# Attention and a gated MLP on one core: transposing the probabilities by VectorE and memory in place of TensorE

## The chip, the cores and the metric

One core of one Trainium2 chip runs the whole program. The metric is the device time of one execution in microseconds (us). The engines named below are TensorE (PE; its weight loads are PEld), VectorE (DVE), ScalarE (ACT), GpSimd (POOL) and SyncE (SP), which here only issues transfers.

## What is computed

Input x has 16 sequences of 256 tokens with 256 features. A layer norm, causal attention with 16 heads of 128 features, a layer norm of its result and a residual add give x1; a layer norm, a gated MLP with dequantised 4-bit weights, a layer norm and a residual add give the output. All of it is fp32.

```
q = einsum(norm(x), W_Q) + b_Q      # k and v likewise
scores = where(causal, q @ k.T / sqrt(128), -100000)
attn = softmax(scores)
z = attn @ v
x1 = x + norm(einsum(z, W_O) + b_O)
gate, up = norm(x1) @ Wg.T, norm(x1) @ Wu.T     # Wg, Wu, Wd = nibble table x scale
out = x1 + norm((gelu(gate) * up) @ Wd.T)
```

## The kernel before

The 4096 tokens are worked in 8 chunks of 512 tokens, two sequences (b = 0, 1) each. Attention is a loop over 8 chunks and 16 heads, 128 steps; then the MLP is a loop over 8 chunks and 16 tiles of its hidden width. Products are made from two fp32r parts of each operand, a high one (rounded) and a low one (the rest): `three` (L487) issues high x high, high x low, low x high. So every operand is split after it is made: ScalarE writes the high part from PSUM, VectorE the low part (the `full` helpers: high at L370 and L372, low at L667 and L669).

The order of the attention loop is the table that `step_plan` (L63) writes; every engine walks through the same table and does its share of each entry. Step j of a chunk holds: q and k of head j + 1; pT, the transposition of head j's probabilities by TensorE, three 128x128 blocks for each b, (L581) into PSUM, split by ScalarE (L445) and VectorE (L831); in steps 0, 4, 8 and 12 the v projections of four heads (four token tiles of 24 products in all); out, the product of head j - 1 with W_O, summed in two PSUM banks over all heads; the scores of head j + 1 (L510, L513 and `three`); and z of head j. Causality leaves three of four 128x128 blocks of scores for each b: queries 0 to 127 with keys 0 to 127, queries 128 to 255 with all keys. In z the early keys meet all 256 queries, the late keys the late 128 queries.

After the scores VectorE adds the mask, scales and takes the row maximum (`mask_scores`, L675 and L679), ScalarE takes the exponentials with their sums (`exps`, L378 and L380), VectorE inverts the sums (L686) and GpSimd multiplies (`normalise`, L953). Both b have one tile of probabilities each, `probs[b]`.

Beside this VectorE has other work at fixed places (`extra`): in steps 1, 3, 5, 7, 9 and 11 it turns nibbles into MLP weights (L736 to L753; the scaling L753 stands behind z's low part), in others it takes the statistics of the next chunk, standardises the last chunk's attention output and adds its residual. ScalarE and GpSimd split these weights too (L392, L947), and ScalarE's queue stores them. The transposes of the next chunk's x (xT, L504) come in step 14. At a chunk's end VectorE takes the summed output from PSUM (L848).

In the first chunk GpSimd splits the attention weights as they come, in 32 pairs of 256 KB (`PAIRS`, both parts on GpSimd, L973 and L975) through two buffers; SP loads a pair when the one before the last is split. SP's queue also loads and stores x, and in the last chunk it loads the dequantised weights.

PSUM: three banks in rotation for q, k, z, v and xT (`fbank`), three for scores and transposed probabilities (`ubank`), two for out (`obank`).

## Time and profile before

| | us |
|---|---|
| median of 3 runs (1725.49 to 1727.16) | 1726.49 |
| the profiled execution | 1724.96 |
| its span | 1723.1 |
| PE busy | 1690.0 (98%) |
| DVE busy | 1210.9 (70%) |
| ACT busy | 928.3 (54%) |
| POOL busy | 518.3 (30%) |
| granted TensorE clock, share of full speed | 0.998 |

The profile is of one execution on the chip. Times in it are us from the start of the span unless marked ns. A matmul's busy time reaches into the next one's, since they are pipelined; the distance of two starts is what an instruction costs. "idle before" is the engine's own idle time just ahead of an instruction, with the engine and line that ended it.

### The profile page before, as it was taken

How to read it: one execution, taken by the hardware profiler on the slowest of the kernel's cores; microseconds unless marked ns; L12 is line 12 of the kernel's file. 1: busy time of each engine (PE TensorE's matmuls, PEld its weight loads, DVE VectorE, ACT ScalarE, POOL GpSimd, SP SyncE). 2: the span in 40 equal slices, each digit the busy share in tenths (PEclk: the TensorE clock that was granted, in tenths of full speed). 3: DMA queues.
4: the chain of work that ended last, by engine and by line, in shares of the span. 5: the costliest groups of instructions: out<-in, count | busy, mean ns of one | idle time of the engine just before them, and what ended most of it. 6: DMA issues, size and time to landing. Idle time of an engine off the chain costs nothing.

```text
span 1723.1 us, 29141 instructions
## 1 busy us (share of the span) xinstructions
PE 1690.0 (98%) x10624; PEld 1506.7 (87%) x10624; DVE 1210.9 (70%) x3488; ACT 928.3 (54%) x2273; POOL 518.3 (30%) x825
## 2 busy tenths in 40 slices
PE   6999999999999999999999999999999999999997
PEld 5998899889899889988989988998888888888886
DVE  5777777777777677777778767876565565566564
ACT  3665566565566556656656656664444444444443
POOL 6662222222122222212212212223333333333332
PEclk9999999999999999999999999999999999999999
DMA  3220011010001001101100102242000000100000
GB/s 118 84 85 22 14 50 32 10 47 20 19 22 50 22 13 50 32 10 47 32 7 22 50 22 86 88 162 73 13 25 22 29 25 13 37 25 13 25 25 13
DMA packets 60239, 67.05 MB, mean 39 GB/s; under 512 B 4672, under 2 KB 53952, under 8 KB 60096
## 3 DMA queue, kind: packets, MB, share of 16 engines
q1 hardware_dynamic: 32832, 46.30, 8.5%
q10 hardware_dynamic: 27264, 18.89, 3.4%
q8 instruction: 85, 1.39, 0.3%
q14 instruction: 58, 0.48, 0.1%
HBM read 44.20 MB, written 20.97 MB: 38 GB/s over the span
## 4 chain that ended last, share of the span: by engine, by line
PE 97%; DVE 1%; ACT 1%; issue 0%; POOL 0%; DMA 0%; POOLq 0%; DVEq 0%; ACTq 0%
PE fbank L488 17%; PE fbank L490 17%; PE fbank L489 17%; PE obank L488 7%; PE obank L489 7%; PE obank L490 7%; PE ubank L488 6%; PE ubank L489 5%; PE ubank L490 5%; PE ubank L581 5%; PE ubank L510 2%; PE ubank L513 1%; PE fbank L504 1%; DVE v_lo L667 0%; DVE zT_lo L669 0%; DVE stream L700 0%
## 5 line engine op out<-in xcount | busy, mean ns | idle before, releaser
L953 POOL TENSOR_SCALAR probs<-probs,rsum 128x128 f32<-128x128 f32 (+1 forms) x512 | 216.7, 437 | 727.0 <-DVE rsum L686 722.0
L488 PE MATMUL fbank<-xnT_hi,weights 128*128 128x512 f32 x768 | 310.5, 404 | 1.4 <-DVE xnT_lo L667 1.4
L490 PE MATMUL fbank<-xnT_hi,weights 128*128 128x512 f32 x768 | 304.4, 396 | 0.0
L489 PE MATMUL fbank<-xnT_lo,weights 128*128 128x512 f32 x768 | 303.9, 396 | 0.0
L378 ACT ACTIVATE probs<-probs,nmax 128x128 f32<-128x128 f32 x256 | 101.0, 394 | 252.1 <-DVE nmax L679 252.1
L404 ACT ACTIVATE w_raw<-fbank 128x512 f32<-128x512 f32 x128 | 76.5, 597 | 265.2 <-PE fbank L490 265.2
L490 PEld LDWEIGHTS fbank<-xnT_hi,weights 128*128 128x128 f32 x768 | 144.5, 188 | 34.6
L488 PEld LDWEIGHTS fbank<-xnT_hi,weights 128*128 128x128 f32 x768 | 145.1, 189 | 25.4 <-DVE xnT_lo L667 1.8
L777 DVE SCALAR_TENSOR_TENSOR w_raw<-w_raw,fbank 128x512 f32<-128x512 f32 x128 | 87.9, 687 | 111.7 <-ACT w_raw L404 111.6
L489 PEld LDWEIGHTS fbank<-xnT_lo,weights 128*128 128x128 f32 x768 | 145.2, 189 | 23.8
L783 DVE SCALAR_TENSOR_TENSOR probs<-w_raw,fbank 128x512 f32<-128x512 f32 x128 | 87.9, 687 | 97.6 <-ACT w_raw L408 97.6
L488 PE MATMUL obank<-wo_hi,zT_hi 128*128 128x256 f32 x512 | 151.7, 296 | 2.4 <-DVE zT_lo L669 2.4
L489 PE MATMUL obank<-wo_lo,zT_hi 128*128 128x256 f32 x512 | 143.3, 280 | 0.0
L490 PE MATMUL obank<-wo_hi,zT_lo 128*128 128x256 f32 x512 | 143.0, 279 | 0.0
L489 PE MATMUL fbank<-pT_lo,v_hi 128*128 128x256 f32 (+1 forms) x512 | 142.5, 278 | 0.0
L490 PE MATMUL fbank<-pT_hi,v_lo 128*128 128x256 f32 (+1 forms) x512 | 142.1, 278 | 0.0
L667 DVE TENSOR_TENSOR v_lo<-fbank,v_hi 128x512 fp32r<-128x512 f32 x128 | 88.5, 691 | 73.8 <-ACT v_hi L370 73.6
L488 PE MATMUL fbank<-pT_hi,v_hi 128*128 128x256 f32 (+1 forms) x512 | 137.4, 268 | 2.7 <-DVE v_lo L667 2.3
L990 POOL TENSOR_TENSOR qT<-probs,qT 128x512 fp32r<-128x512 f32 x64 | 82.9, 1295 | 176.5 <-ACT qT L413 176.5
L372 ACT ACTIVATE kT<-fbank,bias_k 128x512 fp32r<-128x512 f32 x128 | 88.0, 688 | 87.3 <-PE fbank L490 87.3
L669 DVE SCALAR_TENSOR_TENSOR kT<-fbank,bias_k,kT 128x512 fp32r<-128x512 f32 x128 | 96.1, 750 | 53.2 <-ACT kT L372 51.7
L669 DVE SCALAR_TENSOR_TENSOR zT_lo<-fbank,bias_v,zT_hi 128x512 fp32r<-128x512 f32 x128 | 96.1, 750 | 50.5 <-ACT zT_hi L372 50.4
(109 smaller groups left out, 4946.1 us busy)
## 6 DMA issues: line engine op xcount, KB each, us to landing
w_raw<-in_w_pairs SPq DMA_DIRECT2D x32, 256.0 KB, 2.7
weights<-w_hi_scratch SPq DMA_DIRECT2D x8, 768.0 KB, 4.8
weights<-w_lo_scratch SPq DMA_DIRECT2D x8, 768.0 KB, 6.6
x_in<-in_x SPq DMA_DIRECT2D x8, 512.0 KB, 3.8
x_res<-in_x SPq DMA_DIRECT2D x8, 512.0 KB, 5.6
x_scratch<-stream SPq DMA_DIRECT2D x8, 512.0 KB, 3.2
x_in<-x_scratch SPq DMA_DIRECT2D x8, 512.0 KB, 3.8
x_res<-x_scratch SPq DMA_DIRECT2D x8, 512.0 KB, 4.6
```

Of the source, the lines that this page charges most:

```text
L372: ins = act.activation(dst, bank, ACT.Identity, bias=bias)
L378: act.activation(pr[:, 0:P], pr[:, 0:P], ACT.Exp, bias=nmax[:, 0:1], scale=-1.0, accum_out=sums[:, 0:1])
L488: nc.tensor.matmul(out, a[0], b[0], start=start, stop=False, skip_group_check=skip)
L489: nc.tensor.matmul(out, a[0], b[1], start=False, stop=False, skip_group_check=skip)
L490: return nc.tensor.matmul(out, a[1], b[0], start=False, stop=stop, skip_group_check=skip)
L581: last = nc.tensor.transpose(bank[:, t * P:(t + 1) * P], pr[:, t * P:(t + 1) * P], mem.ident[:])
L667: ins = dve.tensor_tensor(dst, bank, hi.bitcast(F32), ALU.subtract)
L669: ins = dve.scalar_tensor_tensor(dst, bank, bias, hi.bitcast(F32), ALU.add, ALU.subtract)
L777: dve.scalar_tensor_tensor(mem.th[j % 2], mem.th[j % 2], 1.0 / GELU_A, mem.gbank[slot(j)][:], ALU.add, ALU.mult).then_inc(s.arg, 1)
L783: after(dve.scalar_tensor_tensor(act_v, mem.th[j % 2], 1.0, mem.gbank[slot(j)][:], ALU.add, ALU.mult))
L953: last = pool.tensor_scalar(pr[:, lo:hi], pr[:, lo:hi], mem.rsum[i][b][:, part:part + 1], 1.0, ALU.mult, ALU.mult)
L990: pool.tensor_tensor(lo, mem.act_v[j % 2], hi.bitcast(F32), ALU.subtract).then_inc(s.iT_lo, 1)
```

## The change

`step_plan` is now numbered over all 128 steps (n = 16 x chunk + head), and one part step is added at the end. Step n holds: q of head n + 1; **T** of head n; k of head n + 1; pT of head n - 1; out of head n - 2; the scores of head n + 1; z of head n - 1; then the v projections. So z and the sum into out come one step later than before, and the scores stand ahead of z and v.

T: VectorE turns each 32x32 block of `probs[b]` (128x384, twelve blocks) into the tile `turned[b]`. SP stores it to memory and, when the store has landed, loads it back in four transfers for each b, one for each group of 32 partitions, in runs of 96 numbers, so that the blocks also change places (`send_around`). `back` has two buffers for each b. pT: ScalarE copies the early keys (256 columns) to the high part, GpSimd writes the low part, both from SBUF. The late keys (128 columns) are used from `back` as they are, in fp32, with `v_late`, an fp32 copy of v's late token tiles; one fp32 product takes the place of three fp32r products. VectorE no longer writes a low part for these tiles or for pT.

Also: the high parts of the attention weights are made by ScalarE and only the low ones by GpSimd; the pairs are in another order and are spread over the steps 0 to 13, two a step, behind four at the start; `x1_norm`'s roots and two residual parts are moved; a nibble tile has one buffer where it had two; the residual, x and weight transfers of SP stand between the round trips; the MLP's first tiles are rearranged.

```diff
-def step_plan(c, j):
+def step_plan(n):
...
-    plan = [("gu", 0)] if last else [("q", j + 1), ("k", j + 1)]
-    plan += [("pT", j)]
-    if j == HEADS - 2:
+    plan = [("q", n + 1), ("T", n), ("k", n + 1)]
+    if n > 0:
+        plan += [("pT", n - 1)]
+    if n % HEADS == HEADS - 2:
         plan += [("xT", 0)]
-    if j % HG == 0:
+    if n > 1:
+        plan += [("out", n - 2)]
+    if n % HEADS == HEADS - 2:
+        plan += [("xT", 1)]
+    plan += [("scores", n + 1)]
+    if n > 0:
+        plan += [("z", n - 1)]
+    if n % HG == 0:
         plan += [("v", t) for t in range(TT)]
...
+    def send_around(n):
+
+        i = n % 2
+        for b in range(2):
+            if n >= 2:
+                sp.wait_ge(s.back[b], 64 * (n - 1))
+            sp.wait_ge(s.turned[b], n + 1)
+            sp.dma_start(turned_v[i][b].rearrange("a i k c -> (a i) k c"),
+                         mem.turned[b][:].rearrange("p k u j -> p k (u j)")).then_inc(s.sent[b], 16)
+        if n >= 2:
+            sp.wait_ge(s.full, nth(("z", n - 2)))
+        for b in range(2):
+            sp.wait_ge(s.sent[b], 16 * (n + 1))
+            for k in range(4):
+                sp.dma_start(mem.back[i][b][32 * k:32 * k + 32].rearrange("p a u j -> p a (u j)"),
+                             turned_v[i][b][:, :, k].rearrange("a i c -> i a c")
+                             ).then_inc(s.back[b], 16)
...
+    for n in range(STEPS_ALL):
+        c, j = n // HEADS, n % HEADS
+        send_around(n)
+        for pair in pairs_of_step(n + 1):
+            load_pair(pair)
+        if c and j == 8:
+            finish(c)
...
         elif kind == "pT":
             for b in range(2):
-                u = 2 * (c * HEADS + m) + b
-                act.wait_ge(s.pT, u + 1)
-                act.activation(mem.pT[b][0][:], mem.ubank[u % UB][:, 0:384],
+                act.wait_ge(s.back[b], 64 * (m + 1))
+                act.activation(mem.pT[b][0][:].rearrange("p (u a j) -> p u a j", a=4, j=32),
+                               mem.back[m % 2][b][:, :, 0:2, :].rearrange("p a u j -> p u a j"),
                                ACT.Copy).then_inc(s.pT_hi, 1)
+            for pair in pairs_of_step(n):
+                weights_hi(pair)
...
                 if u >= UB:
-                    pe.wait_ge(s.pT_lo, u - UB + 1)
+                    pe.wait_ge(s.masked, u - UB + 1)
                 scores(u, h % 2, b)
-        elif kind == "pT":
-            for b in range(2):
-                u = 2 * (c * HEADS + m) + b
-                bank, pr = mem.ubank[u % UB], mem.probs[b]
-                pe.wait_ge(s.probs, u + 1)
-                for t in range(3):
-                    last = nc.tensor.transpose(bank[:, t * P:(t + 1) * P], pr[:, t * P:(t + 1) * P],
-                                               mem.ident[:])
-                last.then_inc(s.pT, 1)
...
-                three(bank[:, o:o + SEQ], [p[:, 2 * b, e0:e0 + E] for p in mem.v],
-                      [p[:, 0:SEQ] for p in mem.pT[b]], True, False)
-                last = three(bank[:, o + P:o + SEQ], [p[:, 2 * b + 1, e0:e0 + E] for p in mem.v],
-                             [p[:, SEQ:384] for p in mem.pT[b]], False, True)
+                three(bank[:, o:o + SEQ], [p[:, b, e0:e0 + E] for p in mem.v],
+                      [p[:] for p in mem.pT[b]], True, False)
+                last = nc.tensor.matmul(bank[:, o + P:o + SEQ].rearrange("p (a j) -> p a j", j=32),
+                                        mem.v_late[:, b, e0:e0 + E], mem.back[m % 2][b][:, :, 2, :],
+                                        start=False, stop=True)
...
-        elif kind == "pT":
+        elif kind == "T":
             for b in range(2):
-                u = 2 * (c * HEADS + m) + b
-                dve.wait_ge(s.pT_hi, u + 1)
-                dve.tensor_tensor(mem.pT[b][1][:], mem.ubank[u % UB][:, 0:384],
-                                  mem.pT[b][0][:].bitcast(F32), ALU.subtract).then_inc(s.pT_lo, 1)
-            if last_head:
-                gated(0, 0)
+                dve.wait_ge(s.probs, 2 * m + b + 1)
+                if m:
+                    dve.wait_ge(s.sent[b], 16 * m)
+                dve.transpose(mem.turned[b][:].rearrange("p k u j -> p u k j"),
+                              mem.probs[b].rearrange("p (u k j) -> p u k j", u=3, k=4)
+                              ).then_inc(s.turned[b], 1)
```

How the rows move. VectorE, a step with nibble work (head 1), from the second inverted sum on, before:

```order
L686 RECIPROCAL rsum<-sums 128x2
L669 SCALAR_TENSOR_TENSOR zT_lo<-fbank,bias_v,zT_hi 128x512
L753 SCALAR_TENSOR_TENSOR w<-spread,scale 128x128 x2
L669 SCALAR_TENSOR_TENSOR qT<-fbank,bias_q,qT 128x512
L669 SCALAR_TENSOR_TENSOR kT<-fbank,bias_k,kT 128x512
L831 TENSOR_TENSOR pT_lo<-ubank,pT_hi 128x384 x2
```

and with the change:

```order
L788 RECIPROCAL rsum<-sums 128x2
L771 SCALAR_TENSOR_TENSOR zT_lo<-fbank,bias_v,zT_hi 128x512
L855 SCALAR_TENSOR_TENSOR w<-spread,scale 128x128 x2
L771 SCALAR_TENSOR_TENSOR qT<-fbank,bias_q,qT 128x512
L935 STREAM_TRANSPOSE turned<-probs 128x3x4x32 x2
L771 SCALAR_TENSOR_TENSOR kT<-fbank,bias_k,kT 128x512
```

The two operations on the probabilities stand between q's and k's low parts, where they stood behind k's. TensorE, one batch half of z and the first product of the next q, before:

```order
L488 MATMUL fbank<-pT_hi,v_hi 128x256
L489 MATMUL fbank<-pT_lo,v_hi 128x256
L490 MATMUL fbank<-pT_hi,v_lo 128x256
L488 MATMUL fbank<-pT_hi,v_hi 128x128
L489 MATMUL fbank<-pT_lo,v_hi 128x128
L490 MATMUL fbank<-pT_hi,v_lo 128x128
L488 MATMUL fbank<-xnT_hi,weights 128x512
```

and with the change:

```order
L595 MATMUL fbank<-pT_hi,v_hi 128x256
L596 MATMUL fbank<-pT_lo,v_hi 128x256
L597 MATMUL fbank<-pT_hi,v_lo 128x256
L695 MATMUL fbank<-back,v_late 128x128
L595 MATMUL fbank<-xnT_hi,weights 128x512
```

Three products of 128 columns have become one. SP's queue in a step of the first chunk, with the change (before, such a step held the w_raw transfers alone):

```order
L398 DMA turned_scratch<-turned 128x384 [waits probs0_turned,turned0_back]
L398 DMA turned_scratch<-turned 128x384 [waits probs1_turned,turned1_back]
L405 DMA back<-turned_scratch 32x4x96 [waits turned0_stored,full_ready]
L405 DMA back<-turned_scratch 32x4x96 x3
L405 DMA back<-turned_scratch 32x4x96 [waits turned1_stored]
L405 DMA back<-turned_scratch 32x4x96 x3
L380 DMA w_raw<-in_w_pairs 128x512 [waits w_split] x2
```

Ten transfers of a round trip stand ahead of the pair loads.

## Rows read from the trace of the kernel before

**Rows 1.** Page, part 1 (busy us, share, instructions) and part 4 (chain by engine)
```profile
PE 1690.0 (98%) x10624; PEld 1506.7 (87%) x10624; DVE 1210.9 (70%) x3488; ACT 928.3 (54%) x2273; POOL 518.3 (30%) x825
...
PE 97%; DVE 1%; ACT 1%; issue 0%; POOL 0%; DMA 0%; POOLq 0%; DVEq 0%; ACTq 0%
```

**Rows 2.** Timeline of one step; start us, us, engine, line, operation, names, shape, [idle <-releaser]
```profile
826.70 0.28 PE L510 MATMUL ubank<-kT,qT 128*128 128x256 f32 x1
...
827.87 0.29 PE L488 MATMUL fbank<-pT_hi,v_hi 128*128 128x256 f32 x1
...
828.22 0.22 PE L488 MATMUL fbank<-pT_hi,v_hi 128*128 128x128 f32 x1
...
828.51 0.33 PE L488 MATMUL fbank<-pT_hi,v_hi 128*128 128x256 f32 x1
...
829.20 0.45 PE L488 MATMUL fbank<-xnT_hi,weights 128*128 128x512 f32 x1
...
830.83 0.75 DVE L669 SCALAR_TENSOR_TENSOR zT_lo<-fbank,bias_v,zT_hi 128x512 fp32r<-128x512 f32 x1 [0.25 <-ACT zT_hi L372]
...
831.50 0.48 DVE L753 SCALAR_TENSOR_TENSOR w<-spread,scale 128x128 f32<-128x128 f16 x2
...
831.90 0.74 DVE L669 SCALAR_TENSOR_TENSOR qT<-fbank,bias_q,qT 128x512 fp32r<-128x512 f32 x1
832.04 0.82 PE L581 MATMUL ubank<-ident,probs 128*128 128x128 f32 x6
832.25 0.69 ACT L372 ACTIVATE kT<-fbank,bias_k 128x512 fp32r<-128x512 f32 x1 [0.71 <-PE fbank L490]
...
832.62 0.36 PE L488 MATMUL obank<-wo_hi,zT_hi 128*128 128x256 f32 x1
...
832.97 0.75 DVE L669 SCALAR_TENSOR_TENSOR kT<-fbank,bias_k,kT 128x512 fp32r<-128x512 f32 x1 [0.32 <-ACT kT L372]
...
834.12 0.28 PE L510 MATMUL ubank<-kT,qT 128*128 128x256 f32 x1
```

**Rows 3.** Two windows, 16 steps and one v step; columns: stretch, us, busy (count), clock, DMA
```profile
683.48:826.70 143.22, 142.53 (x939) 128.59 (x938) 109.41 (x362) 85.67 (x232) 34.09 (x74) 1.00 0.10 29
841.53:854.46 12.93, 12.93 (x78) 11.35 (x77) 9.65 (x30) 7.28 (x18) 3.67 (x7) 1.00 0.07 21
```

**Rows 4.** Timeline, a step without nibble work
```profile
819.27 0.28 PE L510 MATMUL ubank<-kT,qT 128*128 128x256 f32 x1
...
824.15 0.75 DVE L669 SCALAR_TENSOR_TENSOR qT<-fbank,bias_q,qT 128x512 fp32r<-128x512 f32 x1
```

**Rows 5.** Groups of instructions by form; busy us, mean ns of one, idle before
```profile
L831 DVE TENSOR_TENSOR pT_lo<-ubank,pT_hi 128x384 fp32r<-128x384 f32 x256 | 129.5, 547 | 0.3 <-ACT pT_hi L445 0.3
...
L975 POOL TENSOR_TENSOR weights<-w_raw,weights 128x512 fp32r<-128x512 f32 x24 | 31.2, 1302 | 2.0
```

**Rows 6.** Timeline of the start
```profile
20.89 0.75 DVE L669 SCALAR_TENSOR_TENSOR kT<-fbank,bias_k,kT 128x512 fp32r<-128x512 f32 x1 [0.62 <-ACT kT L372]
...
21.70 0.39 PE L510 MATMUL ubank<-kT,qT 128*128 128x256 f32 x1 [1.56 <-DVE kT L669]
...
40.41 0.28 PE L510 MATMUL ubank<-kT,qT 128*128 128x256 f32 x1
```

**Rows 7.** Timeline where one chunk ends and the next begins
```profile
727.03 0.37 PE L510 MATMUL ubank<-kT,qT 128*128 128x256 f32 x1
...
727.95 0.69 DVE L667 TENSOR_TENSOR xnT_lo<-fbank,xnT_hi 128x512 fp32r<-128x512 f32 x1 [0.67 <-ACT xnT_hi L370]
...
740.59 1.27 DVE L848 TENSOR_TENSOR stream<-obank,bias_o 128x512 f32<-128x512 f32 x2
```

**Rows 8.** DMA issues: what, queue, count, KB each, median us from issue to landing
```profile
w_raw<-in_w_pairs SPq DMA_DIRECT2D x32, 256.0 KB, 2.7
...
w_lo_scratch<-w_0lo ACTq DMA_DIRECT2D x24, 128.0 KB, 2.3
```

**Rows 9.** Timeline of SP's queue at the start
```profile
1.22 0.96 SPq L319 DMA_DIRECT2D w_raw<-in_w_pairs  x2
```

More of the change, by code:

```diff
@@ new lines, with whole, full_key @@
+STEPS = [(n, kind, m) for n in range(STEPS_ALL + 1) for kind, m in step_plan(n)]
+FULLS = ("q", "k", "v", "z", "xT")
+LAST_Z = ("z", STEPS_ALL - 1)
+def whole(kind, m):
+    return kind == "v" and m % 2 == 1
+def full_key(n, kind, m):
+    if kind == "xT":
+        return (kind, n // HEADS + 1, m)
+    if kind == "v":
+        return (kind, n // HG, m)
+    return (kind, m)
+def full_places():
+    place = {("xT", 0, 0): 0, ("xT", 0, 1): 1, ("q", 0): 2, ("k", 0): 3}
+    gates, late, at = {}, [], len(place)
+    for n, kind, m in STEPS:
+        if kind == "gu" and m < 2:
+            gates[m] = at
+            at += 1
+        elif kind in FULLS:
+            key = full_key(n, kind, m)
+            if key == LAST_Z:
+                at = place["z", m - 1] + FB
+            if whole(kind, m):
+                late.append(at)
+            place[key] = at
+            at += 1
+    return place, gates, late
@@ L113, in nth, with split, copied @@
 def nth(key):
+    return ORDER[PLACE[key]] + 1
+def split(key):
     return SPLITS[PLACE[key]] + 1
[L118 to L120 removed]
+def copied(key):
+    return COPIES[PLACE[key]] + 1
 class Memory:
```

384 lines of the change are left out of this document (206 added, 178 removed).

## The prediction

> **What bounds the kernel now.** I read the page's busy times first, then the chain that ended last, then one step instruction by instruction. TensorE is busy for 98% of the span and is 97% of the chain [rows 1]; a wait such as the one before L510 at 21.70, 1.56 us for VectorE's kT [rows 6], is found at the start, and the chain has no share of VectorE above 1%. So TensorE's own instructions set the pace: a step (one head of one chunk) repeats after 7.42 us, from the first score matmul at 826.70 to the next at 834.12 [rows 2], and the 16 steps from 683.48 to 826.70 take 143.22 us, the four with the v projections mostly 12.93 us (841.53 to 854.46) [rows 3]. The reader is to see how little stands behind that. Between q low (831.90) and k low (832.97) VectorE has a gap; k low starts 0.03 us after ScalarE's kT ends, is over at 833.72, and the scores start at 834.12, only 0.40 us later [rows 2]. Whatever lengthens that way by more than 0.40 us becomes the pace.
>
> **What leaves TensorE.** Six transposes go: 832.04 to 832.62, 0.58 us a step, 74 us over 128 steps [rows 2]. In z each batch half loses three 128-column products, 828.22 to 828.51, 0.29 us, and the 256-column product behind them starts 0.05 us late (0.17 instead of 0.12 us) [rows 2]: 0.34 us twice. In their place stands one product of 128 columns whose operands, v_late and back, are plain fp32. No row shows one. Bounds: an fp32 transpose through TensorE, 0.58 / 6 = 0.097 us [rows 2]; above, two 512-column products, 2 x 0.235 = 0.47 us (829.20 to 832.04 holds the twelve of q and k) [rows 2]. I take 0.37, a little over the three products of the same two operands that it replaces, since it carries the same product at full precision. So z grows from 1.33 (827.87 to 829.20) to about 1.39 us. If TensorE alone set the pace, a plain step would be scores 1.17 + z 1.39 + q and k 2.84 + out 1.50 = 6.9 us.
>
> The Trainium skill (FP8 and Floating Point Precision, "TensorE Precision Notes") says that true fp32 takes four passes through the array. Four times 0.097 would be an estimate of 0.39 us; no run here shows the product, and by it the sum would be 2 us higher.
>
> **What is added to VectorE's path.** The order of VectorE becomes z low, (nibble work), q low, two 32x32 turns of 128x384, k low. Before, pT low stood behind k low, where nobody waited for it before z; now the turns stand in front of k low, and the scores wait for k low. No row shows a turn. The nearest is pT low with the same 384 elements, 0.547 us each [rows 5]. An instruction gives way 0.08 us before its own end (z low lasts 0.75, the next starts 0.67 after it [rows 2]), so a pair holds VectorE for 0.93 us. Bounds for a pair: 0.80 us, four nibble scalings of 128 elements (two take 831.50 to 831.90), though these hold 512 elements and the pair 768; and 1.5 us, two q lows, if a 4-byte turn is not streamed [rows 2]. I take 0.93.
>
> Now one step from the first score matmul, time 0 [rows 2]. After the masks, ScalarE's four exponentials and z high, z low starts at 4.13, the scaling of the nibbles at 4.80, q low at 5.20. None of this moves: it hangs on the scores themselves. From there: q low 0.67 + turns 0.93 + k low 0.75 + 0.06 to the matmul (kT ended at 20.89 + 0.75, L510 started at 21.70 [rows 6]) = 7.61 us. The step was 7.42. That is a step with nibble work (six in a chunk). Without it q low starts at 824.15 - 819.27 = 4.88 [rows 4], so 7.29 us. A second way leads there through q itself: q's last product issued, 0.21 to ScalarE, 0.69, 0.03, q low, turns, k low: with z at 1.33 it gives 4.88 too, with 1.39 us it gives **7.35**. A v step is that plus the v projections, 12.93 - 7.42 = 5.51: 12.86.
>
> A chunk in segments after each step's scores: steps 2, 6, 15: 3 x 7.35 = 22.1. Step 10 has the moments before q low: 7.5. Step 13 is bound by TensorE, 6.9 us and eight transposes of x at 0.1: 7.7. Step 14: xnT low runs ahead of the masks, 0.73 later (it occupies VectorE until 1.6 us after the scores at 727.03): 8.0 [rows 7]. Steps 3, 5, 9, 11: 4 x 7.61 = 30.4. Step 7 has a residual add between the nibble operations (half of L848's 1.27 us [rows 7], part of it hidden): 8.0. Step 1: the output of the previous chunk is now taken from PSUM before the masks, 1.27 us after a wait for out [rows 7]: 8.4. Four v steps 51.4. Sum 143.5 against 143.22 us. **The 74 us on TensorE are eaten by the wait before the scores**: 8 x 0.3 = +2 us, and -1 for chunk 0, which has no residual work.
>
> **The edges.** Start: POOL splits four pairs before its first normalise, and pair 3 is loaded only when pair 1 is split; ScalarE copies pairs 1 to 3 ahead of the first exponentials. Chained with 1.3 us for a split (L975), 2.7 for a load and 0.6 for a copy the second step's scores go to about 44.0 where they were at 40.41 [rows 5, 6, 8]: +3.5. z and out come one step later, so one head of them (1.4 + 1.5) lies behind the last step, less its 0.58 of transposes: +2.3. The last head's way through memory is in the open: +2.5. In the last chunk the 768 KB loads of the MLP weights (three times a weight pair's 256 KB and 2.7 us [rows 8]) stand on the queue of the round trips: five places, +3. Together 11 us.
>
> **The round trip**, hidden if it fits. Turns end at 6.1 and 6.6; SP issues two in 0.96 us [rows 9]; a store of 128 KB lands 2.3 us after its issue [rows 8], so the first has landed at 8.4 and SP's eight loads are issued from 8.4 to 12.2; the last lands at 14.0. ScalarE's copy of 256 elements takes some 0.4 (its 512 of k take 0.69 [rows 2]), POOL's low part 0.65 (half of L975 [rows 5]): 15.1. z wants it at 2 x 7.35 + 1.17 + 0.7 = 16.5. 1.4 us are free. SP issues ten transfers, 4.8 us of 7.35. ScalarE waits for the return in front of the exponentials, which are due after 2 x 7.35 + 1.66. Residual and x transfers come behind v steps, which have 5.5 us more. POOL's step is 1.7 us of normalising, 1.3 of pT low and 0.7 for a nibble tile, in chunk 0 2.6 of splits more: it fits.
>
> **Sum.** The profiled execution of before took 1724.96 us (span 1723.1), the median is 1726.49. 1725.0 + 1 + 11 = 1737 as profiled, 1738 against the median.
>
> **Rivals.**
> *Short turns* (not slower). If the pair of turns takes 0.80 and the fp32 product 0.25 us, plain steps are 7.16, nibble steps 7.48, v steps 12.5: some 140.2 a chunk, 8 x 3.0 = -24 us, and + 11 for the edges: 1713. For it: a turn reads and writes SBUF alone, pT low read PSUM. Against it: 0.80 is the time of 512 elements, and the pair has 768. It decides from a pair of about 0.80 together with a product below 0.3 us; short turns alone give 1722.
> *TensorE stays the bound*, the turns finding a gap that I don't see: 6.9 and 12.4 us, 132.6 a chunk: 1651. Against it speaks the chain of [rows 2].
> *Dear fp32 product*, 0.47 us or a pair of turns of 1.1: z 1.6, plain 7.56, nibble 7.78, v 13.1: +20 to 35 on the forecast: 1765.
> *Late return.* If a transfer takes 3 us instead of 2, two legs are 1.4 us longer, all that is free; with 3.5 us every z waits 1 us more: 1738 + 128 = 1866, and 1790 at 3.2 us. For it: 1024 pieces of 384 bytes a step, of which before has none. The Trainium skill (VectorE: DVE Perf Modes, "The three transpose paths") warns that a plain DMA used as a transpose is 19 times slower where the destination's innermost stride is large. Here each piece is a run of 96 numbers, and the turning inside a block is VectorE's; by that rule taken in full the time would be this rival's or worse, and no row of this case shows such a transfer.
>
> **Chances.** Forecast 0.45 (1724 to 1752), dear product or turn 0.22, short turns 0.20, late return 0.08, TensorE the bound 0.05. A measurement of this kernel can tell about 0.2% (3.5 us) from no change. The range 1706 to 1790 takes in the second and third and the near end of the fourth. Faster: 0.22; within 0.2%: 0.13, from the low end of the forecast; slower: 0.65.
>
> **What would show it.** TensorE below 95% busy, with its matmul L620 waiting for kT low in nearly every step, 0.3 to 0.7 us; VectorE's turns at 0.5 us, directly behind q low; steps of about 7.35, 7.6 and 12.9 us; L548 on ScalarE seldom waiting for the return. The working is wrong if the steps stand at 6.9 us, if L620 waits for nothing, or if pT low (L1085) is what z waits for.

## The result, and the profile after

The changed kernel takes **1750.45 us** (median; 1746.33 to 1754.67), the kernel before 1726.26 us (1725.49 to 1727.16): a ratio of 1.014, 95% interval 1.0114 to 1.0166. It is slower, as forecast, and within the stated range of 1706 to 1790, but by 24 us where the forecast said 12. The profiled execution is the fastest of the four, 1746.33 us with a span of 1744.5, so the traces explain 21.4 us (1744.5 - 1723.1).

From the page of the changed kernel: busy times, the chain by engine, two groups and the landing times of the new transfers.

```profile
PE 1618.9 (93%) x9600; PEld 1408.5 (81%) x9600; DVE 1161.0 (67%) x3424; ACT 919.2 (53%) x2305; POOL 678.2 (39%) x1049
...
PE 55%; DVE 25%; ACT 11%; issue 4%; DMA 2%; SPq 1%; POOL 0%; ACTq 0%; DVEq 0%; POOLq 0%
...
L620 PE MATMUL ubank<-kT,qT 128*128 128x256 f32 x256 | 85.7, 335 | 87.0 <-DVE kT L771 87.0
...
L935 DVE STREAM_TRANSPOSE turned<-probs 128x384 f32<-128x384 f32 x256 | 131.6, 552 | 0.3 <-DMA turned_scratch<-turned 0.3
...
turned_scratch<-turned SPq DMA_DIRECT2D x256, 192.0 KB, 2.2
back<-turned_scratch SPq DMA_DIRECT2D x1024, 48.0 KB, 1.9
```

TensorE is busy for 93% of the span instead of 98%, the chain has VectorE and ScalarE in it [rows 1 had 97% of PE], and L620, the first score matmul, waits 87 us for k low (6.6 of it once, at the start of the second step). 71 us of TensorE's work have left (1690.0 - 1618.9), and more than that has come back as waits.

One plain step of it, from the first score matmul at 487.43 to the next at 494.71 (timeline; start and duration in us), which is [rows 2, 4] of before:

```profile
487.43 0.39 PE L620 MATMUL ubank<-kT,qT 128*128 128x256 f32 x1 [0.96 <-DVE kT L771]
...
489.06 0.39 PE L695 MATMUL fbank<-back,v_late 128*128 128x128 f32 x2
...
489.21 0.36 PE L595 MATMUL fbank<-pT_hi,v_hi 128*128 128x256 f32 x1
...
490.96 0.67 ACT L471 ACTIVATE zT_hi<-fbank,bias_v 128x512 fp32r<-128x512 f32 x1
...
491.67 0.75 DVE L771 SCALAR_TENSOR_TENSOR zT_lo<-fbank,bias_v,zT_hi 128x512 fp32r<-128x512 f32 x1 [0.34 <-ACT zT_hi L471]
...
492.33 0.74 DVE L771 SCALAR_TENSOR_TENSOR qT<-fbank,bias_q,qT 128x512 fp32r<-128x512 f32 x1
...
492.87 0.69 ACT L471 ACTIVATE kT<-fbank,bias_k 128x512 fp32r<-128x512 f32 x1 [0.67 <-PE fbank L597]
...
492.99 1.03 DVE L935 STREAM_TRANSPOSE turned<-probs 128x384 f32<-128x384 f32 x2
...
493.94 0.71 DVE L771 SCALAR_TENSOR_TENSOR kT<-fbank,bias_k,kT 128x512 fp32r<-128x512 f32 x1
...
494.71 0.38 PE L620 MATMUL ubank<-kT,qT 128*128 128x256 f32 x1 [0.46 <-DVE kT L771]
```

The two turns hold VectorE from 492.99 to 493.94, 0.95 us. k high is ready at 493.56 (492.87 + 0.69), and k low could start then; it starts at 493.94, ends at 494.65, and the scores follow at 494.71. The step is 7.28 us, and nibble steps and v steps are 7.68 and 12.66. The fp32 product starts at 489.06 and the next one 0.15 us later.

By stages (windows: stretch, us, busy time and count of PE, PEld, DVE, ACT, POOL, granted clock, DMA share, GB/s): the first chunk, the third, and the last up to its last scores.

```profile
20.26:174.24 153.98, 131.97 (x765) 112.95 (x765) 104.33 (x334) 98.00 (x258) 92.26 (x133) 0.97 0.53 154
316.88:459.52 142.64, 132.56 (x809) 115.70 (x809) 102.33 (x352) 82.31 (x232) 56.74 (x107) 1.00 0.42 117
1030.58:1169.94 139.36, 126.50 (x764) 110.06 (x765) 96.58 (x334) 77.46 (x218) 53.70 (x101) 1.00 0.53 155
```

| stretch | before | after | difference | forecast |
|---|---|---|---|---|
| to the second step's scores | 40.41 | 44.16 | +3.75 | +3.5 |
| rest of the first chunk | 123.13 | 130.08 | +6.95 | -1 |
| chunks 2 to 7 | 858.92 | 856.34 | -2.6 | +2 |
| last chunk, to its last scores | 134.02 | 139.36 | +5.3 | +3 |
| from there to the end | 566.62 | 574.56 | +7.9 | +4.8 |

(Each entry is a difference of two starts of L510 before and L620 after; the first chunk ended at 163.54 before and at 174.24 after. The forecast is the prediction's: +2 for the chunks, -1 for the first, which has no residual work.) So the steady chunks, on which most of the working was spent, came out right, and the loss lies where no steady step runs.

### The profile page after: what moved, and what is told of

It reads as the page before. It is cut to its first block, busy times and chain, and to the rows that moved or that the text cites. A ratio compares the mean times of both kernels' runs of the same rounds, so it can differ in the third digit from the quotient of the medians.

```text
span 1744.5 us, 29181 instructions
## 1 busy us (share of the span) xinstructions
PE 1618.9 (93%) x9600; PEld 1408.5 (81%) x9600; DVE 1161.0 (67%) x3424; ACT 919.2 (53%) x2305; POOL 678.2 (39%) x1049
## 4 chain that ended last, share of the span: by engine, by line
PE 55%; DVE 25%; ACT 11%; issue 4%; DMA 2%; SPq 1%; POOL 0%; ACTq 0%; DVEq 0%; POOLq 0%
PE fbank L595 9%; PE fbank L597 9%; PE fbank L596 9%; DVE turned L935 6%; PE ubank L595 5%; PE ubank L597 4%; PE ubank L596 4%; DVE kT L771 4%; ACT probs L478 4%; PE obank L597 4%; PE obank L595 4%; PE obank L596 4%; ACT probs L476 3%; DVE probs L781 3%; DVE zT_lo L771 3%
## 5 line engine op out<-in xcount | busy, mean ns | idle before, releaser
L1085 POOL TENSOR_TENSOR pT_lo<-back,pT_hi 128x256 fp32r<-128x256 f32 x256 | 183.3, 732 | 384.3 <-ACT pT_hi L548 383.8
L620 PE MATMUL ubank<-kT,qT 128*128 128x256 f32 x256 | 85.7, 335 | 87.0 <-DVE kT L771 87.0
L499 ACT ACTIVATE w_raw<-fbank 128x512 f32<-128x512 f32 x88 | 52.5, 597 | 191.9 <-PE fbank L597 191.9
L595 PE MATMUL obank<-wo_hi,zT_hi 128*128 128x256 f32 x512 | 146.8, 287 | 5.8 <-DVE zT_lo L771 4.6
L777 DVE TENSOR_TENSOR probs<-ubank,mask 128x128 f32<-128x128 f32 x256 | 73.9, 289 | 108.4 <-PE ubank L597 108.1
L771 DVE SCALAR_TENSOR_TENSOR qT<-fbank,bias_q,qT 128x512 fp32r<-128x512 f32 x128 | 95.2, 744 | 74.1 <-ACT qT L471 74.1
L596 PE MATMUL obank<-wo_lo,zT_hi 128*128 128x256 f32 x512 | 143.0, 279 | 0.0
L1073 POOL TENSOR_TENSOR kT<-probs,kT 128x512 fp32r<-128x512 f32 x64 | 82.7, 1292 | 154.8 <-ACT kT L508 154.8
L620 PEld LDWEIGHTS ubank<-kT,qT 128*128 128x128 f32 x256 | 48.4, 189 | 112.2 <-DVE kT L771 112.2
L935 DVE STREAM_TRANSPOSE turned<-probs 128x384 f32<-128x384 f32 x256 | 131.6, 552 | 0.3 <-DMA turned_scratch<-turned 0.3
L478 ACT ACTIVATE probs<-probs,nmax 128x256 f32<-128x256 f32 x256 | 126.5, 494 | 0.0
```

Of the source, the lines that this page charges most:

```text
L478: act.activation(pr[:, P:384], pr[:, P:384], ACT.Exp, bias=nmax[:, 1:2], scale=-1.0, accum_out=sums[:, 1:2]).then_inc(s.exp, 1)
L595: nc.tensor.matmul(out, a[0], b[0], start=start, stop=False, skip_group_check=skip)
L596: nc.tensor.matmul(out, a[0], b[1], start=False, stop=False, skip_group_check=skip)
L620: nc.tensor.matmul(bank[:].rearrange("p (r e) -> p r e", e=P)[:, 0:4:3, :], q[0][:, o:o + P], k_both[:, :, o:o + P], start=True, stop=Fals ...
L771: ins = dve.scalar_tensor_tensor(dst, bank, bias, hi.bitcast(F32), ALU.add, ALU.subtract)
L935: dve.transpose(mem.turned[b][:].rearrange("p k u j -> p u k j"), mem.probs[b].rearrange("p (u k j) -> p u k j", u=3, k=4)).then_inc(s.tur ...
```

## Experiments: is it the turns' place?

**Turns behind k low.**

```diff
-    plan = [("q", n + 1), ("T", n), ("k", n + 1)]
+    plan = [("q", n + 1), ("k", n + 1), ("T", n)]
```

> The changed kernel with VectorE's two turns behind k low instead of in front of it (and the next masks waiting for the turn of the same b, since both touch probs). My theory: the turns in front of k low are what the scores wait for. Then k low starts 0.03 us behind kT high (6.06 after the scores), a plain or nibble step is 6.83 us (now 7.28 and 7.68), a v step 12.2 (now 12.66), a chunk 133 (now 142.6): 1746 - 78 = 1668 us, if the round trip were free. It isn't: the turns then end 1.1 us later, and from the end of a turn to pT low are 8.7 us by the trace of the change, so z of head n waits where two steps together are under 14.7 us; that is about 1 us in each group of four steps, +32: about 1700 us, with L595 (z) waiting for pT low 20 to 40 us in all. Rival, no gain: the return is late in every step, steps settle at 7.35 us, 1745. Rival, the wait before the scores has another cause than the turns: 1746 and L620 waits 80 us as now.

1749.78 us, ratio 1.0142 (1.0125 to 1.0159): no gain, where about 1700 was forecast. The trace shows why. L620's wait fell from 87.0 to 27.6 us. Steps in which the return was in time took 6.87 and 6.97 us, v steps 12.50: the turns' place is what bounded them. But many others took 7.1 to 9.3 us, a few over 10, and chunks stayed at 140.5 to 144. Its groups of the first score matmul and of pT high, then one late step in the timeline:

```profile
L620 PE MATMUL ubank<-kT,qT 128*128 128x256 f32 x256 | 85.2, 333 | 27.6 <-DVE kT L771 26.3
...
L548 ACT ACTIVATE pT_hi<-back 128x256 fp32r<-128x256 f32 x256 | 101.4, 412 | 134.1 <-DMA back<-turned_scratch 134.1
```

```profile
495.30 0.42 ACT L548 ACTIVATE pT_hi<-back 128x256 fp32r<-128x256 f32 x1 [1.11 <-DMA back<-turned_scratch]
...
496.68 0.36 PE L595 MATMUL fbank<-pT_hi,v_hi 128*128 128x256 f32 x1 [0.22 <-POOL pT_lo L1087]
...
497.16 0.42 ACT L548 ACTIVATE pT_hi<-back 128x256 fp32r<-128x256 f32 x1 [1.44 <-DMA back<-turned_scratch]
...
498.43 0.39 PE L595 MATMUL fbank<-pT_hi,v_hi 128*128 128x256 f32 x1 [0.93 <-POOL pT_lo L1087]
```

ScalarE waits 134 us for the return (33.9 in the change), and since pT high stands ahead of the exponentials, they start late too; z waits at 496.68 and 498.43. My sum of the loop (14.7 us from a turn's end to pT low and round to the next turn) fits this, my account of how often it bites was too small: a late step lengthens ScalarE's way as well, so the gain of one step is lost in the next.

**One more turn.** `for b in (1, 0, 1)`: b = 1 is turned twice, with a wait between instructions that write the same tile.

> The changed kernel with the turn of b = 1 done twice, so three turns in front of k low. Turns-bound theory: each step but step 14 grows by one turn, 0.48 to 0.6 us (with the wait between two turns of one tile): plain 7.8, nibble 8.2, v 13.2 us; 120 x 0.5 = 60 us: 1806. Rival (what limits the steps is the return, the clock or a contention): under 15 us more.

1831.95 us, 1.061 (1.0594 to 1.0625): 81.5 us more than the change. Plain steps 7.99, nibble steps 8.40, v steps 13.38: 0.71 us each, 0.56 for a turn and the rest for the waits between them. The direction is that of the forecast, the size above its 60 us, which had 0.5 for a step. L620's idle time rose by 84.6 us:

```profile
L620 PE MATMUL ubank<-kT,qT 128*128 128x256 f32 x256 | 86.6, 338 | 171.6 <-DVE kT L771 171.6
```

**No fp32 product** (L695 left out, so z lacks the late keys).

> The changed kernel without the fp32 product of the late keys (left out of z; the early keys' three products stay), two products a step. My reading of the trace: z ends long before ScalarE, busy with the exponentials, takes it up (3.53 us after the scores), so the product's 0.15 us twice is hidden: 0 to 3 us less in all. Rival, the forecast's second way through z and q: 0.3 us of every step, 1746 - 38 = 1708.

1748.12 us (1.011 to 1.014): nothing that can be told from the change, as forecast. A chunk is 142.33 instead of 142.64, the wait before L620 92.8 us instead of 87.0. The product costs 0.15 us of TensorE's pace (1.63 to 1.78 us after the scores of the step shown above), and that is hidden behind the exponentials: z's last product has been issued by 2.4, and ScalarE takes z up at 3.53.

**Both b in one store and four loads**, first with the turns in their place, then behind k low. One tile `turned` and one `back` for both b:

```diff
-        for b in range(2):
-            sp.wait_ge(s.sent[b], 16 * (n + 1))
-            for k in range(4):
-                sp.dma_start(mem.back[i][b][32 * k:32 * k + 32]...
+        sp.wait_ge(s.sent[0], 16 * (n + 1))
+        for k in range(4):
+            sp.dma_start(mem.back_both[i][32 * k:32 * k + 32]...
```

> The changed kernel with both b in one store and four loads a step (5 transfers where there were 10; the tile turned and each back one tile for both b). The round trip of b = 1 gets about 1.3 us shorter, SP's issues 2.3 us a step instead of 4.6. Turns-bound theory: nothing in the steady steps waits for the return, so a chunk stays at 142.6; ScalarE's wait for the return (33.9 us) goes, and chunk 0 and chunk 7, where pair and weight loads share SP's queue, give back 2 to 6 us: 1740 to 1745. Return theory (the trip bounds steps now): a chunk drops by over 2 us, below 1730. Against both: one store that waits for both turns and moves 384 KB lands later, 1755.

> Both of the last two edits: turns behind k low, and both b in one store and four loads. If the turns' place is the wait and the late return all that stands in its way, steps are 6.83 us and v steps 12.2, a chunk 133: about 1668 us, faster than before by 3.4%; TensorE over 96% busy, L620 waiting for kT low under 20 us. If the return is still late, 1680 to 1700. If another way is next (masks held by the turn, exponentials), 1690 or more with DVE or ACT named ahead of L777.

1746.99 (1.0103 to 1.0133) and 1751.03 us (1.0125 to 1.0155). Half the issues on SP's queue give back 3.5 us (1740 to 1745 was forecast for the first); for the second the forecast of 1668 fell. The steady chunks of the first stayed at 142.7 to 143.0 us, so the return sets no steady step of the change. Its first chunk fell from 154.0 to 151.4 us, by 0.9 us in step 4 and 1.4 in step 12. The joined store lands after 2.5 us and the loads after 2.4, where they took 2.2 and 1.9, and the store waits for both turns. So fewer issues bought little.

**k low between the turns.** The first turn keeps its place, since the store of b = 0 opens the round trip, and the loads of b = 1 stand behind those of b = 0 anyway.

```diff
         elif kind == "T":
-            for b in range(2):
+            for b in range(1 if n < STEPS_ALL - 1 else 2):
                 turn(m, b)
...
             elif kind == "k":
                 full(count, mem.kT[h % 2][1], ...)
+                turn(n, 1)
```

> The changed kernel with k low between the two turns: q low, turn of b = 0, k low, turn of b = 1 (and the masks of a b waiting for its turn). With both turns behind k low the steps fell to 6.87 and 6.97 us wherever the return was in time, but in the others z waited for pT low and the chunks stayed at 142.7: SP can begin the first loads only when the first store has landed, and that store was 0.9 us later. Here the first turn keeps its place, so its loads start as in the changed kernel, and those of b = 1 queue behind them anyway. One turn in front of k low fits into the 0.49 us between q low and k low of a plain step and costs a nibble step 0.4. Forecast: plain 6.85 to 6.95, nibble 7.2 to 7.3, v 12.2 to 12.5 us, a chunk 135.5 to 137, total 1690 to 1700. Rival, the return is the next bound even so (the two-step loop is 14.7 us): 1735 to 1750 with ScalarE's pT high waiting over 100 us.

1725.66 us, 0.9993 (0.9983 to 1.0002): 25 us below the change, level with before. Steps are 6.97, 7.23 and 12.5 us, a chunk 138.0, and L620 waits 47.9 us where it waited 87.0 (its group on the page; then the windows of the seventh and the last chunk):

```profile
L620 PE MATMUL ubank<-kT,qT 128*128 128x256 f32 x256 | 85.6, 334 | 47.9 <-DVE kT L771 46.6
```

```profile
868.07:1006.11 138.04, 132.72 (x809) 115.95 (x809) 103.79 (x353) 82.58 (x232) 56.97 (x107) 1.00 0.43 121
1006.11:1149.10 142.99, 131.52 (x764) 114.01 (x765) 98.75 (x335) 77.99 (x218) 53.84 (x101) 0.95 0.52 152
```

So the order of two instructions on VectorE made 39 of the 87 us of that wait, and held 4.6 us of each chunk. I had forecast 1690 to 1700; a chunk came out at 138.0 us where 135.5 to 137 was forecast, and the first chunk took 156.7 and the last 143.0 us.

**The scaling of the nibbles behind k low** in addition:

> As the last, and the nibbles' scaling, which stands behind z low, moved behind k low. If VectorE's order in front of k low is all that keeps a nibble step above a plain one, nibble steps are 6.9 to 7.0 too and the total is 10 to 15 us below that of the kernel before it. Rival: the second turn and with it the return come 0.4 us later, z waits in a third of the steps, and the total is not better.

1727.51 us (0.9999 to 1.0017). Nibble steps fell to 6.97 us, and the v steps behind them rose to 13.1 in most chunks, where TensorE now waits 0.3 us for z low or for pT low. The total is not better, which was the rival.

## Experiments: the first and the last chunk

**Four buffers for the weight pairs** (two in the tile of the residual):

> The changed kernel with four buffers for the weight pairs where it had two (the other two in the tile of the residual, which is now loaded at the start of the second chunk), so that loads run ahead of their splits. Theory 1: the first chunk is long (154.0 us against 142.6 in the later ones) because pairs are loaded late, and ScalarE's high parts wait for them ahead of the exponentials: the first chunk falls by 5 us or more, the total to 1737 to 1741. Theory 2: it is the added work of ScalarE and GpSimd (one high, one low part twice a step) and not the loads: under 2 us, 1745 or more.

1749.07 us (1.0114 to 1.0144). The first step fell from 10.8 to 7.4 us, as its pairs are loaded sooner; the others didn't. Late loads of pairs are 3.4 us of the first chunk; the total can't be told from the change's.

The nibble steps there take 8.33 us where later ones take 7.68. In the trace of the change (VectorE's first nibble operation and GpSimd's splits):

```profile
84.14 1.29 POOL L1063 TENSOR_TENSOR weights<-w_raw,weights 128x512 fp32r<-128x512 f32 x1
...
84.53 0.98 DVE L838 TENSOR_SCALAR spread<-words 128x128 int32<-128x128 int32 x1
...
85.55 0.29 DVE L840 SCALAR_TENSOR_TENSOR spread<-words,spread 128x128 int32<-128x128 int32 x1
```

The answer on its line (count, ns min/median/max, first and last start):

```profile
L838 DVE TENSOR_SCALAR spread<-words x48: 220/225/1076, 46.9 to 1142.8; 128x128 int32<-128x128 int32 x48
```

L838 takes 0.98 us, where its median of 48 is 0.225, and it ends 0.08 us after GpSimd's operation has. The Trainium skill (SBUF — State Buffer, "Who interferes with whom") says that VectorE and GpSimd share a pair of ports and that the second one waits for the whole instruction of the first. To see whether this operation or VectorE's work as such is held, **L838 was left out in the first chunk** (so six weight tiles are made without it):

> The changed kernel without the first of the nibble operations (L838) in the first chunk (left out there: its six weight tiles come out wrong). In that chunk L838 takes 0.6 to 1.1 us where it takes 0.22 elsewhere, and ends 0.08 us after an operation of GpSimd ends; the nibble steps there are 8.33 us and more against 7.69. Theory: GpSimd's splits hold this operation, and it holds the step: nibble steps of the first chunk fall to 7.5 (7.69 less the 0.22 us), the chunk by 4 to 5 us, the total to 1742. Rival (late loads or ScalarE's copies): over 8.1 us, total unchanged. If the hold passes on to the next operation (L840), it is VectorE's work as such that GpSimd holds, and the steps stay too.

```profile
85.23 1.29 POOL L1065 TENSOR_TENSOR weights<-w_raw,weights 128x512 fp32r<-128x512 f32 x1
...
85.64 1.04 DVE L841 SCALAR_TENSOR_TENSOR spread<-words,spread 128x128 int32<-128x128 int32 x1
```

1750.46 us (1.0123 to 1.0155), nibble steps 8.06 (the two that had 8.33 before, and others from 7.87 to 8.89): only about the operation's own share, 0.27 us, went, and the next one (L841 here, L840 in the change), which took 0.29 us behind L838, now takes 1.04 and ends 0.16 us after GpSimd's. The hold passes on. It agrees with the page, which counts both forms (one that can run in a two-port mode, one with two SBUF inputs) among those that are held. The masks, which read PSUM, are not held beside the same splits: in this step they take the 0.29 and 0.41 us that they take everywhere. Nor is every operation on SBUF alone held: a turn that started at 28.42, in the middle of such a split, took 0.54 us.

All six L838 of this chunk are held until 0.08 or 0.09 us after a split's end, and in steps 7 and 11 L840 runs into the next split too. Step 11:

```profile
137.12 2.53 POOL L1063 TENSOR_TENSOR weights<-w_raw,weights 128x512 fp32r<-128x512 f32 x2
...
137.78 0.71 DVE L838 TENSOR_SCALAR spread<-words 128x128 int32<-128x128 int32 x1
138.52 1.28 DVE L840 SCALAR_TENSOR_TENSOR spread<-words,spread 128x128 int32<-128x128 int32 x1
```

In steps 3, 5, 7, 9 and 11 these holds add 0.86, 0.76, 1.52, 0.76 and 1.48 us to VectorE's work, and the steps are 0.74, 0.64, 1.40, 0.64 and 1.36 us longer than 7.69, a later nibble step without residual work. The two rows agree within 0.12 us in every step. No run took the splits away from beside these operations, so the price rests on this agreement.

The kernel before had such holds too, at another place. GpSimd split more there (both parts), but the splits stood clear of L736, which took 0.22 us in every step, and met the scaling L753 in five steps, where the first of its two operations took 0.75 us instead of 0.28:

```profile
80.45 0.95 DVE L753 SCALAR_TENSOR_TENSOR w<-spread,scale 128x128 f32<-128x128 f16 x2
80.45 0.62 POOL L973 TENSOR_SCALAR weights<-w_raw 128x512 fp32r<-128x512 f32 x1
```

The steps around them took 7.44 and 12.93 us, as in later chunks, since TensorE was the bound.

**The MLP weights' loads.** In the last chunk of the change, two loads of 768 KB (L374) are issued at 1098.62, and the store of turned probabilities behind them (L398, 1100.04) is followed by its loads (L405) only at 1106.56, 6.5 us later; ScalarE waits 3.63 us.

```profile
1098.62 0.38 SPq L374 DMA_DIRECT2D weights<-w_hi_scratch  x1
...
1099.04 0.43 SPq L374 DMA_DIRECT2D weights<-w_lo_scratch  x1
...
1100.04 0.94 SPq L398 DMA_DIRECT2D turned_scratch<-turned  x2
...
1106.56 4.45 SPq L405 DMA_DIRECT2D back<-turned_scratch  x8
...
1110.88 0.42 ACT L548 ACTIVATE pT_hi<-back 128x256 fp32r<-128x256 f32 x1 [3.63 <-DMA back<-turned_scratch]
```

The DMA engines, busy for 0.42 of a steady chunk, are busy for 0.92 of the time between these issues:

```profile
1098.62:1106.56 7.94, 7.42 (x47) 6.24 (x45) 6.85 (x24) 4.32 (x14) 3.56 (x7) 1.00 0.92 289
```

Is it the queue that they share? **The loads on ScalarE's queue**, alone and with k low between the turns:

```diff
-            sp.dma_start(mem.w4_all[part][:, 6 * q:6 * q + 6]...
+            act.dma_start(mem.w4_all[part][:, 6 * q:6 * q + 6]...
```

> The changed kernel with the loads of the MLP weights (768 KB each) issued on ScalarE's queue, at the same steps, where SP's queue issued them among the round trips. In the trace of the change the store of turned probabilities that is issued 1 us behind two of these loads (step 7 of the last chunk) takes about 6 us until its loads go out, where such a store otherwise takes 2.2, and steps 8, 9, 11 and 12 are 4.7 us longer than in the other chunks. Theory (the queue they share): the last chunk falls to 134.7 us for its 15 steps (from 139.4 in the fastest run and over 143 in others), total 1740 to 1742, and the runs lie closer together. Rival (the 16 DMA engines are full whatever the queue): the last chunk stays over 139.

> Both edits: k low between the turns, and the MLP weights on ScalarE's queue. The former had a chunk of 138.0 us, but its last chunk took 143.0 and its first 156.7. With the shared queue as the cause the last chunk falls to about 130.5: 1725.7 - 12.5 = 1713 us, faster than before by 0.8%. Rival (DMA engines full): 1722 or more.

1768.60 us (1.0231 to 1.0265) and 1737.35 us (1.0047 to 1.0077): worse by 18 and 12 us, and the theory of the shared queue fell. Of the 22 us between the first one's profiled span and the change's, 16 lie behind the last scores. From the first of the two (ScalarE's queue, SP's queue, ScalarE, and TensorE near the end):

```profile
1127.80 0.32 ACTq L490 DMA_DIRECT2D weights<-w_hi_scratch  x1
...
1128.15 0.46 ACTq L490 DMA_DIRECT2D weights<-w_lo_scratch  x1
...
1128.37 0.81 SPq L387 DMA_DIRECT2D turned_scratch<-turned  x2
...
1135.57 3.67 SPq L394 DMA_DIRECT2D back<-turned_scratch  x8
...
1202.37 0.42 ACT L544 ACTIVATE pT_hi<-back 128x256 fp32r<-128x256 f32 x1 [12.60 <-DMA back<-turned_scratch]
...
1203.73 0.55 PE L595 MATMUL fbank<-pT_hi,v_hi 128*128 128x256 f32 x1 [13.48 <-POOL pT_lo L1085]
```

The store at 1128.37 stands on another queue than the loads at 1127.80, and its own loads still begin 7.2 us later; the DMA engines were busy for 0.92 of that time. The last round trip, behind eight loads of 768 KB issued together, keeps TensorE waiting 13.48 us. The Trainium skill (DMA: Bandwidth & Descriptors, "Issuing engines are not separate DMA queues") says that transfers run on the same 16 DMA engines whoever issues them; this case agrees, with 7.2 us on two queues and 6.5 on one.

**The loads in pieces of 256 KB**, two behind each round trip from step 1 to 15 (the last six loads stay large), with the turns in either order:

```diff
-                if j == min((6 * q + 5) // 2, HEADS - 2) + 1:
-                    load_w4(q)
+            if j:
+                load_w4(j - 1)
+            if j == HEADS - 1:
+                for q in range(5, NT // 2):
+                    load_w4(3 * q, 6)
```

> The changed kernel with the MLP weights of the last chunk loaded in pieces of 256 KB, two behind each round trip of SP's queue, instead of 1.5 MB at five places. On ScalarE's queue the big loads held the returns up as well, so it isn't the queue: theory now, a transfer of 768 KB keeps all 16 DMA engines for its 4 to 7 us and a round trip issued behind it waits, whatever the queue. In pieces it waits 1.5 to 3 us at most, about what is free. Last chunk 136 us for its 15 steps (from 139.4 to 143), total 1741 to 1744 and a smaller spread. Rival (the bytes are what counts, 12 MB in one chunk): last chunk 140 or more, 1746 or more.

> The same pieces in the kernel with k low between the two turns (1725.7, last chunk 143.0). With the return free: last chunk 131 to 133, total 1714 to 1716, faster than before by 0.6%. If the pieces, 1.8 us of issues a step on SP's queue and 2.9 us of transfer, make the return late in most steps (it has some 0.3 us free there): 1722 or more.

1748.98 us (1.0115 to 1.0144) and 1720.83 us (0.9954 to 0.9979). With the change's own order the last chunk took 138.06 us where 136 was expected, and the total can't be told from the change's 1750.45; with k low between the turns it is 4.8 us below the 1725.66 of the same kernel with large loads, and 0.3% faster than before (1714 to 1716 was forecast). So large transfers at few places cost more than small ones at every step where the return has little time to spare; size and spreading were changed together, and no run tells them apart. The pieces are not free either: 15 clean steps would take 134.7 us in the first (142.64 - 7.9) and some 130.5 in the second, whose profiled last chunk was 138.7. In the second the v steps carry most of it (up to 16.3 us instead of 12.5); in the first they carry half (13.2 and 13.3 instead of 12.7) and one nibble step 1.3 us.

**Pair loads on ScalarE's queue**, with four buffers, the MLP loads there too, k low between the turns:

> As the last, with four buffers for the weight pairs and their loads on ScalarE's queue, a step ahead, so that SP's queue carries little but round trips. Four buffers alone took 3.4 us from the first step and nothing from the later ones. If the pair loads on SP's queue hold the returns up in the first chunk as the MLP weights do in the last, the first chunk falls from 156.7 to about 146: 1702 us. If GpSimd's and ScalarE's added work makes the first chunk long: 153 or more there, 1709.

1743.57 us (1.0087 to 1.0117), the first chunk 157.1 us where 146 or 153 was forecast: moving the pairs to another queue gave nothing there either.

**k low between the turns, small loads, four buffers:**

> As the last, with four buffers for the weight pairs; these took 3.4 us from the first step of the changed kernel and nothing elsewhere. 3 us below the kernel before it: 1711 to 1713. If the first chunk is set by GpSimd, which holds VectorE's nibble operation (and, with the first left out, the second: 1.04 us in place of 0.29), the gain of the first step is given back within the chunk: within 1 us of the kernel before it.

**1715.43 us** (1713.52 to 1718.62), ratio 0.9937 (0.9925 to 0.9949): faster than both kernels, by 0.6% against the kernel before. Its windows of the first, third and last chunk:

```profile
19.87:170.17 150.30, 131.14 (x765) 111.37 (x765) 105.08 (x334) 97.63 (x258) 92.27 (x133) 0.99 0.52 150
308.48:447.05 138.57, 132.89 (x808) 115.92 (x808) 103.66 (x353) 82.52 (x233) 57.18 (x107) 1.00 0.43 120
1000.61:1135.91 135.30, 127.15 (x764) 110.32 (x765) 98.97 (x335) 78.43 (x218) 53.78 (x101) 1.00 0.56 162
```

Here the first step's 3.3 us are kept, and the profiled last chunk is 3.4 us shorter than that of the run with two buffers. Why it is, with the same loads there, stays open; single executions of these kernels differ by 5 to 9 us.

## Why the prediction was right or wrong

The prediction's terms add up to 12 us, the profiled execution is 21.4 us longer. The term of the first chunk, put at -1 because "it fits", is 8 us too low, the tail's 3.1, the last chunk's 2.3 (1.6 of it by the MLP weights' loads); the steady chunks, 4.6 us too high, hid part of that.

**The turn, and what bounds the step: right.** 0.93 us for a pair was forecast, 0.95 measured; a mean of 552 ns for one. The nearest row was of another operation with as many elements, so the hit is partly luck. L620 waits for k low in 120 of 128 steps, mostly 0.3 to 1.2 us, and with the turns behind k low that wait fell by two thirds. Plain steps 7.28 (7.35 forecast), nibble steps 7.68 (7.61), v steps 12.66 (12.86), step 10 7.55 (7.5), step 13 7.53 (7.7), step 14 7.9 (8.0). Two were off by 0.4 us in opposite directions: step 1, 7.97 (8.4), step 7, 8.38 (8.0). A chunk is 142.64 us (143.5). The 7.35 came from the second way, through q, whose terms as written add up to 7.32; the first way's 7.29 is what was measured. That 74 us on TensorE would be eaten by the wait before the scores held: the chunks lost nothing and gained 0.4 us each.

**The fp32 product: too dear.** 0.37 us forecast, 0.15 measured, so that z takes 1.08 us instead of 1.39. The estimate of 0.39 us from the four passes of the Trainium skill (FP8 and Floating Point Precision, "TensorE Precision Notes") was as far off. It mattered little, since at this price z is hidden (the run without it); it did make the second way through q, and with it the plain and v steps, 0.1 to 0.2 us too long. So the product's part of the rival "dear product" was priced on a way that does not bind here. Two sums of the rivals are off: the v step of "short turns" is 7.16 + 5.51 = 12.67, not 12.5, and two legs of 3 us in "late return" are 1.7 us longer (0.7 and 1.0), not 1.4.

**The first chunk, "it fits": the step that failed most.** Forecast -1 behind the start, measured +6.95 us. I had added up GpSimd's time and found room, and asked neither whom its operations hold nor what waits for loads. In the kernel before, holds of VectorE in this chunk lay in TensorE's shadow; with VectorE the bound, each counts. The six nibble steps are 4.8 us longer than the same steps of later chunks, and this goes with the holds by GpSimd's splits, in steps 3 to 11 within 0.12 us; of step 1's 0.73 us only 0.41 is such a hold. Steps 4 and 12 (13.56 and 14.38 us where later chunks have 12.66) make 2.6. There ScalarE waits for weight pairs (1.01 and 0.32 us in step 4, 0.46 in step 12) and for a return (1.71, at 144.07). With five transfers on SP's queue in place of ten these two steps took 12.70 and 12.99 us, with four buffers 13.72 and 14.73: so it goes with the round trip's transfers and not with the buffers, as far as one profile of each shows. Together 7.4 us, less the 0.45 that a steady chunk gains.

The +3.75 to the second step's scores were forecast as late pairs, and with four buffers these scores stand at 40.40 instead of 44.16. That before had 40.41 is chance: the first scores came 1.4 us earlier than before, and their place differs by up to 1 us among the runs.

**The MLP weights' loads: mis-sized.** +3 forecast as five places on SP's queue, 4.6 measured, in the four segments behind the scores of heads 8, 9, 11 and 12 of the profiled execution (9.18, 14.48, 7.98, 9.27 against 8.38, 12.66, 7.55, 7.69), and more in others: with the same loads the profiled last chunks of the runs without the product and with four buffers took 143.3 and 144.5 us. I priced issues; what counts is the 6 to 7 us for which the DMA engines are full (0.92 busy). Most of the gap between the profiled 1746.33 and the median of 1750.45 is probably this: the four executions' mean granted clocks fall with their times (0.994, 0.992, 0.991, 0.990), as they would with such waits, but of three of them there is no trace.

**The tail: mis-sized.** +4.8 forecast, +7.9 measured. The last head's way was right in kind; TensorE waits four times, 3.9 us where 2.5 was forecast (0.78 us for the head before it, then 0.66, 0.93 and 1.56 for the last; here the last two, and the window of what follows with its granted clock):

```profile
1186.14 0.39 PE L595 MATMUL fbank<-pT_hi,v_hi 128*128 128x256 f32 x1 [0.93 <-POOL pT_lo L1085]
...
1188.55 0.80 PE L595 MATMUL ubank<-xnT_hi,weights 128*128 128x512 f32 x1 [1.56 <-DVE zT_lo L771]
```

```profile
1188.55:1191.70 3.15, 3.15 (x7) 2.51 (x8) 0.00 (x0) 0.18 (x1) 0.00 (x0) 0.50 1.02 420
```

After the last of these waits the clock granted was 0.50, its lower level of 1.2 GHz, for 3.1 us, and a 512-column product took 0.43 us instead of 0.235: 1.3 us that I had not counted.

**The round trip: right.** A store lands after 2.2 us (2.3), loads after 1.9 (2.0). 1.4 us free were forecast; in the fourth chunk pT low of b = 1 ends from 0.03 us before a step's scores to 1.23 behind them, and z takes it up at 1.77, so 0.5 to 1.8 us are free. ScalarE waited 33.9 us for returns in 39 places, but the 17.6 us of it in chunks 2 to 7 cost next to nothing: the steps kept their times, since the exponentials behind it start only 1.8 us after the scores. The rival of a late return did not come true as such, yet with the turns behind k low it ate the whole gain. Short turns and the bound by TensorE did not come true. The 19 times slower transfer of the Trainium skill (VectorE: DVE Perf Modes, "The three transpose paths") was not met: a load of 48 KB in runs of 96 numbers lands after 1.9 us. The page speaks of a large innermost stride at the destination, which these runs don't have, so no run here tests it.

## What to carry over

When work leaves the engine that sets the pace, first ask what in front of its next waiting instruction moves: here one turn of 0.5 us ahead of k low cost as much as the whole change had lost, and swapping two instructions gave 25 us. Then price the stages that are not steady (first chunk, last chunk, tail) one by one against the new bound, for the old bound's shadow hides holds, late loads and returns that now count. A short round trip through memory was held up by a large transfer issued just ahead of it, on either queue tried.

## What the runs showed of the hardware

- A 32x32 turn of 128x384 fp32 takes 552 ns, two in a row 0.95 us.
- An fp32 product of 128 columns leaves two records and costs 0.15 us of TensorE's pace (489.06 to 489.21 in the changed kernel).
- GpSimd's 128x512 subtraction from SBUF (1.28 us) holds VectorE's nibble operations until 0.08 to 0.16 us after its own end: the one with one SBUF input (0.22 became up to 1.08 us) and the one with two (0.29 became up to 1.28). GpSimd's copy L973 does so to the scaling L753 (0.28 became 0.75). The masks, which read PSUM, and a turn were not held.
- Two loads of 768 KB delay a 192 KB store issued 1 us later by over 4 us, from the same queue (6.5 us to the start of its loads instead of about 2.2) or from another (7.2).
- TensorE's granted clock fell to its lower level, 0.50, after the waits of 0.93 and 1.56 us at the attention's end; in the last chunk of the kernel with k low between the turns TensorE waits 1.91 us for the return behind the scores at 1116.28, and the mean clock from there to the next scores was 0.73.
